# A graph layer with residual and layer norm: 417 edge lists of up to 385 nodes instead of 441 of up to 308

## The reference

```
row, col = src, dst
messages = x[col] @ W.T + b
agg      = segment_sum(messages * agg_weight, row, num_segments=100000)
h        = x + agg
out      = (h - mean(h)) / sqrt(var(h) + 1e-5)      # over the 128 features
```

## Time and profile before

| | |
|---|---|
| median of 3 runs | 845.09 us (844.79 to 850.85) |
| profiled execution | 849.63 us |
| its span | 847.9 us |
| VectorE, TensorE busy | 752.7 us (89%), 721.6 us (85%) |
| ScalarE, GpSimd busy | 635.2 us (75%), 590.1 us (70%) |
| mean granted TensorE clock | 0.965 |

### The profile page before, as it was taken

How to read it: one execution, slowest core, us unless ns; L and a number is a source line. 1 busy time by engine, 2 the same in 40 slices (tenths; PEclk the granted TensorE clock), 3 DMA queues, 4 the chain that set the end, 5 groups by cost and what they waited for, 6 DMA issues and landing times.

```text
span 847.9 us, 22961 instructions
## 1 busy us (share of the span) xinstructions
PE 721.6 (85%) x7822; PEld 540.1 (64%) x7849; DVE 752.7 (89%) x2457; ACT 635.2 (75%) x1592; POOL 590.1 (70%) x601
## 2 busy tenths in 40 slices
PE   4889999999997888888887887888879888888875
PEld 4745555555545667777766766767668677666764
DVE  7989999999966889998988998989899889898985
ACT  2157778777823778887887887888788788878878
POOL 3037777776747777777777777777777777777750
PEclk9999999999998998998999999999999999999998
DMA  2001111111042677777777777777777777777773
GB/s 78 14 27 34 35 39 40 41 39 34 9 150 62 199 240 222 226 232 224 223 228 221 230 238 233 228 222 227 240 229 231 218 232 231 233 224 232 226 223 141
DMA packets 81025, 141.11 MB, mean 166 GB/s; under 512 B 19360, under 2 KB 20396, under 8 KB 80908
## 3 DMA queue, kind: packets, MB, share of 16 engines
q1 hardware_dynamic: 62476, 110.55, 39.1%
q0 software_dynamic: 18432, 29.08, 14.4%
HBM read 87.64 MB, written 51.92 MB: 165 GB/s over the span
## 4 chain that ended last, share of the span: by engine, by line
PE 34%; POOL 21%; DVE 16%; issue 13%; DMA 9%; ACT 7%; POOLq 0%; SPq 0%; ACTq 0%; DVEq 0%
POOL xg L522 20%; PE bank L654 10%; DMA xg<-in_x,table 8%; PE bank L732 7%; ACT y L1100 5%; DVE stats L993 3%; DVE sel L977 2%; DVE rest L975 2%; PE bank L603 2%; PE bank L548 2%; DVE xl L980 2%; PE bank L609 2%; PE bank L702 1%; PE bank L706 1%; PE bank L704 1%
## 5 line engine op out<-in xcount | busy, mean ns | idle before, releaser
L522 POOL DMA_INDIRECT xg<-in_x,table x441 | 445.8, 1011 | 143.5 <-issue 130.1
L1100 ACT ACTIVATE y<-h,shift,rstd 128x128 f32<-128x128 f32 x784 | 321.6, 482 | 78.6 <-DVE shift L1004 78.4
L732 PE MATMUL bank<-wT,aggT 128*128 128x128 f32 x1568 | 237.2, 297 | 0.0
L732 PEld LDWEIGHTS bank<-wT,aggT 128*128 128x128 f32 x1568 | 198.9, 199 | 27.0 <-issue 9.0
L702 PE MATMUL bank<-sel,xg 128*128 128x308 bf16 (+11 forms) x685 | 166.5, 256 | 11.6 <-DVE xl L980 6.3
L477 POOL DMA_INDIRECT place_scratch<-word_col,place_row x135 | 135.7, 1005 | 54.6 <-issue 50.4
L704 PE MATMUL bank<-sel,rest 128*128 128x308 bf16 (+11 forms) x685 | 172.5, 255 | 0.0
L706 PE MATMUL bank<-sel,xl 128*128 128x308 bf16 (+11 forms) x685 | 162.8, 255 | 0.0
L993 DVE BATCH_NORM_STATS2 stats<-h 128x6 f32<-128x256 f32 x392 | 147.6, 418 | 0.2
L986 DVE TENSOR_TENSOR h<-bank,xt 128x512 f32<-128x512 f32 x196 | 133.8, 683 | 13.8 <-PE bank L732 12.9
L975 DVE TENSOR_TENSOR rest<-xg 128x384 f32<-128x384 f32 x196 | 88.9, 454 | 51.8 <-DMA xg<-in_x,table 51.6
(11 more groups left out here) (151 smaller groups left out, 787.8 us busy)
## 6 DMA issues: line engine op xcount, KB each, us to landing
xt<-in_x SPq DMA_DIRECT2D x195, 256.0 KB
out<-y SPq DMA_DIRECT2D x195, 256.0 KB, 2.4
xg<-in_x,table POOLq DMA_INDIRECT x441, 3.5
hi_row<-hi_scratch SPq DMA_DIRECT2D x50, 128.0 KB
place_scratch<-word_col,place_row POOLq DMA_INDIRECT x135
place_scratch<-scattered SPq DMA_DIRECT2D x1, 441.0 KB, 3.4
scattered<-place_scratch SPq DMA_DIRECT2D x1, 441.0 KB, 3.3
src_rows<-in_src SPq DMA_DIRECT2D x1, 192.0 KB
```

The costliest lines, as they stand in the source:

```text
L522: nc.gpsimd.indirect_dma_start(out=xg[:, m, k], out_offset=None, in_=x, in_offset=bass.IndirectOffsetOnAxis(ap=table[:, period * LISTS + k ...
L732: last = nc.tensor.matmul(OUT[u % RO][:, nodes[j]], aggT[:, u % RO, nodes[j]], wT[:], start=False, stop=True, skip_group_check=True)
L1100: nc.scalar.activation(y[:, u, j], h[:, u, j], ACT.Identity, bias=shift[:, u, j:j + 1], scale=rstd[:, u, j:j + 1]).then_inc(s_y, 1)
```

## The change

A period is now 4096 nodes (8 groups) with 17 lists, so a list has 241 nodes of its own instead of 228, and its tail is 144 nodes instead of 80. A selection is 385 columns wide (384 for the seventeenth list) instead of 308 or 307. There are 25 periods; the last has four groups, so only nine of its lists exist, and 417 lists are left. Every loop leaves out lists from number `NB` on. `xg` holds 2 periods and `sel`, `rest` and `xl` one, again 16 and 8 groups, and the waits on `s_sum`, `s_out` and `s_agg` ask for the same groups as before. In the last round GpSimd also fetches the list that ends beyond the last group. The lists that begin in a group are 3, 2, 3, 1 in a period before, and 3, 2, 2, 3, 2, 2, 2, 1 after; those that end in it 2, 2, 2, 3 before, and 2 in seven groups and 3 in the eighth after.

```diff
-    SPAN_G, LISTS = 4, 9
+    SPAN_G, LISTS = 8, 17
     SPAN_N = SPAN_G * GN
-    SPAN_BITS = 11
-    PERIODS = GA // SPAN_G
-    NB = LISTS * PERIODS
-    TAIL = 80
+    SPAN_BITS = 12
+    PERIODS = -(-GA // SPAN_G)
+    TAIL = 144
     FIRST = [-(-SPAN_N * k // LISTS) for k in range(LISTS + 1)]
+    NB = LISTS * (PERIODS - 1) + sum(FIRST[k] < (GA - (PERIODS - 1) * SPAN_G) * GN for k in range(LISTS))
...
-    RX = 4
+    RX = 2
+    XR = 1
...
-        sel = sb("sel", [P, 2, LISTS, SW], bf16)
-        rest = sb("rest", [P, 2, LISTS, D])
-        xl = sb("xl", [P, 2, LISTS, D], bf16)
+        sel = sb("sel", [P, XR, LISTS, SW], bf16)
+        rest = sb("rest", [P, XR, LISTS, D])
+        xl = sb("xl", [P, XR, LISTS, D], bf16)
...
-                    for turn, k in enumerate(LAST_IN[u % SPAN_G]):
+                    mine = LAST_IN[u % SPAN_G]
+                    if g == GA - 1:
+                        mine = [k for k in range(mine[0], LISTS) if period * LISTS + k < NB]
+                    for turn, k in enumerate(mine):
                         if period >= RX:
-                            if turn == 0:
-                                pool.wait_ge(s_sum, g - RX * SPAN_G + 1)
+                            if turn == 0 or k not in LAST_IN[u % SPAN_G]:
+                                pool.wait_ge(s_sum, (period - RX) * SPAN_G + (FIRST[k + 1] - 1) // GN + 1)
                             elif turn == 1:
                                 at_least(pool, s_out, g - RX * SPAN_G - 1)
...
-                    parts = PARTS[g % SPAN_G] if g < GA - 1 else PARTS[g % SPAN_G][:-1]
                     period = g // SPAN_G
-                    return [((period + k // LISTS) % RX, (period + k // LISTS) % 2, k % LISTS, slice(lo, hi), slice(at, at + hi - lo))
-                            for k, lo, hi, at in parts]
+                    return [((period + k // LISTS) % RX, (period + k // LISTS) % XR, k % LISTS, slice(lo, hi), slice(at, at + hi - lo))
+                            for k, lo, hi, at in PARTS[g % SPAN_G] if period * LISTS + k < NB]
...
-                    at_least(dve, s_agg, g - (SPAN_G + 2))
-                    mine = CLASS[u % SPAN_G]
+                    at_least(dve, s_agg, g - (XR * SPAN_G - 2))
+                    mine = [k for k in CLASS[u % SPAN_G] if period * LISTS + k < NB]
```

More of the change, by code:

```diff
@@ L66, in gnn_resnorm_kernel @@
     RO = 4
-    RX = 4
+    RX = 2
+    XR = 1
     EPS = 1e-5
-    assert NS > NB and GA % SPAN_G == 0 and 1 << SPAN_BITS == SPAN_N and 1 << LO_BITS == LO and CA <= KB * P and GN == 512 and NB <= 512 and N <= 1 << 17
+    assert NS > NB and 1 << SPAN_BITS == SPAN_N and 1 << LO_BITS == LO and CA <= KB * P and GN == 512 and NB <= 512 and N <= 1 << 17
     ctx = ExitStack()
@@ L342, in rounds @@
                         stage(g, g % R, g // R, g // SPAN_G, g // SPAN_G % RX, g // SPAN_G // RX)
-        assert SPAN_G == RO and R % SPAN_G == 0
+        assert R % SPAN_G == 0 and max(WIDTH) <= GN
         block = ctx.enter_context(nc.Block())
@@ L693, in aggregate @@
                     if u % SPAN_G < SPAN_G - 1:
-                        pe.wait_ge(s_sel, LISTS * period + sum(len(c) for c in CLASS[:u % SPAN_G + 1]))
+                        pe.wait_ge(s_sel, min(NB, LISTS * period + sum(len(c) for c in CLASS[:u % SPAN_G + 1])))
                     elif last_group:
@@ L973, in select @@
                         dve.wait_ge(s_first[m], 16 * mn + 16)
-                    dve.wait_ge(s_rest[m][u % SPAN_G], (16 * mn + 16) * len([k for k in mine if k]))
-                    V.tensor_tensor(rest[:, m % 2, lists], xg[:, m, lists], top[:, m, lists, :, 1], ALU.subtract).then_inc(s_upper, 1)
+                    dve.wait_ge(s_rest[m][u % SPAN_G], 16 * mn * len([k for k in CLASS[u % SPAN_G] if k]) + 16 * len([k for k in mine if k]))
+                    V.tensor_tensor(rest[:, m % XR, lists], xg[:, m, lists], top[:, m, lists, :, 1], ALU.subtract).then_inc(s_upper, 1)
                     for k in mine:
-                        V.tensor_scalar(sel[:, m % 2, k, 0:WIDTH[k]], iota_win[:, WIN[k]:WIN[k] + WIDTH[k]],
+                        V.tensor_scalar(sel[:, m % XR, k, 0:WIDTH[k]], iota_win[:, WIN[k]:WIN[k] + WIDTH[k]],
                                         table[:, period * LISTS + k, 1:2], None, ALU.is_equal).then_inc(s_sel, 1)
                     dve.wait_ge(s_upper, g + 1)
-                    V.tensor_tensor(xl[:, m % 2, lists], rest[:, m % 2, lists], middle[:, m % 2, lists, :, 1], ALU.subtract).then_inc(s_lower, 1)
+                    V.tensor_tensor(xl[:, m % XR, lists], rest[:, m % XR, lists], middle[:, m % XR, lists, :, 1], ALU.subtract).then_inc(s_lower, 1)
                 def add_x(g, u, n, period, m, mn):
```

2 lines of the change are left out of this document (1 added, 1 removed).

## The result

The changed kernel takes 809.74 us (808.70 to 809.88), the kernel before 845.31 us: ratio 0.956, 95% interval 0.953 to 0.959. It is faster, by 35.6 us. The forecast of 815.7 us had the sign and the pacing engine right, but its range, 811 to 824 us, does not reach down to the measured time. Two extra figures are needed to read the traces: the profiled execution after took 808.70 us (span 807.0), 1 us under its median, and that of before 849.63, 4.3 us over its median. So the two traces differ by 40.9 us, the medians by 35.6.

A forecast was written before the change was run, and what follows sets the result against it. GpSimd, issuing gathers without a stop, was taken to bound the main stage. Gathers -30.1, sorting stage -0.5 and drain +1.2 us sum to -29.4, taking the median from 845.09 to 815.7 us; range 811 to 824.

The forecast's parts named there:

- 24 gathers: GpSimd, main stage: 441 gathers become 417, saving 30.1 us (bounds 29 to 31.6).
- The width is hidden: VectorE, main stage: with wider selections it needs 2.68 us a group, covered by GpSimd's 2.79.
- Rings and waits: Main stage: rings hold as many groups and waits ask for the same groups as before, so cost nothing.
- (1): Rival, main stage: VectorE or TensorE takes over the pace; median 818 to 828 us; chance 0.13.
- (2): Rival: the VectorE, ScalarE and TensorE loop already needs the present pace; gain under 8 us, 838 to 845; chance 0.06.
- (3): Rival: 385-wide selections leave the fast form on VectorE, 0.24 us more each; +45 us, about 890; chance 0.04.
- (4): Rival: lists overflow and the serial branch runs, taking over 3500 us; chance 0.01.
- Several signs: Things to check in the profile after: gather period, last gather's start, waits of VectorE and TensorE, selection times, merge start.
- this excess ... stays: GpSimd's gathers: the 26 us beyond 0.952 us each stays, so each removed gather saves only 1.25 us.
- the drain: After the last gather: TensorE sets the pace for some six groups, 0.2 us more each, +1.2 us.
- the stage before: Sorting stage ahead of the gathers: narrower matmuls and one-hot tiles, scatters unchanged; -0.5 us (0 to 1.4 gain).

The follow-up runs named there:

- before_more: Kernel before plus one more gather per group into an unread spare tile, 637 gathers in all: 1090.4 us, ratio 1.290 to the kernel before.
- after_more: Changed kernel plus one more gather per group into an unread spare tile, 613 gathers in all: 1053.4 us, ratio 1.246 to the kernel before.
- narrow_17: Changed kernel with the tail of 80 instead of 144 (417 lists, 321-column selections); two runs, ratios 0.957 and 0.959 to the kernel before.
- form_only: Changed kernel with 18 lists and tail 80: the same 441 lists as the kernel before, in periods of 8 groups; ratios 0.996, 0.997, 0.996 to it.
- before_24_less: Kernel before with 24 of its 441 gathers left out, all else kept; three runs, ratios 0.973, 0.974 and 0.978 to the kernel before.
- wide_only: Changed kernel with 18 lists instead of 17 and its tail of 144 (441 lists): 1101.3 us, ratio 1.000 to the kernel before.
- after_again: Changed kernel run again without an edit: 1076.3 us, ratio 0.956 to the kernel before on the same chip.
- before_again: Kernel before run again without an edit: 1102.1 us, ratio 1.002.
- before_cut: Kernel before with both splits made list by list, 441 short ones each instead of 196: ratio 1.003.
- before_joined: Kernel before with the split xl moved ahead of the selections, right behind the split rest: ratio 1.002.

## Why the prediction was right in kind and too small

**Right.** GpSimd sets the pace, and 24 gathers are most of the gain: shown by before_more against after_more, by narrow_17 against form_only for the lists as a whole, and by before_24_less in part. The width is hidden on VectorE's own path: it needs 2.66 us a group (forecast 2.68), a selection 336 ns (331); the waits left are 21.1 us ("some 20"). Rings and waits changed nothing that GpSimd waits for. Rivals (1), (2) and (3) did not happen, and (4) neither: 417 gathers, no serial branch. Several signs missed their numbers: the period was 1.299 us, not 1.31 to 1.32; the last gather came 40.1 us earlier, not 30; TensorE's waits for ScalarE fell by 44 us, not 30; the merge started at 236.8 us, not 237 to 238.

**Wrong: the term "this excess ... stays".** I took 24 x 1.25 and held the 26 us that gathers take beyond 0.952 constant. It fell. Between the two traces it went from 441 x 0.059 = 26.0 us to 417 x 0.042 = 17.5, 8.5 us. On the medians less of that is left: 35.6 less 30.1 (the 24 gathers at 1.25), 1.4 and 0.8 leaves 3.3 us. The other 5.2 us are about what the two profiled executions stood off their medians (4.3 above and 1.0 below); that it was the gathers' excess that differed there is inferred, since the other executions have no trace. What lengthens a gather can be seen in the trace of before. GpSimd, then VectorE:

```profile
564.58 1.34 POOL L522 DMA_INDIRECT xg<-in_x,table  x1 [0.30 <-issue]
566.23 0.95 POOL L522 DMA_INDIRECT xg<-in_x,table  x1 [0.30 <-issue]
...
568.74 1.19 POOL L522 DMA_INDIRECT xg<-in_x,table  x1 [0.30 <-issue]
```

```profile
564.55 0.55 DVE L980 TENSOR_TENSOR xl<-rest 128x384 bf16<-128x384 f32 x1
...
566.02 0.69 DVE L986 TENSOR_TENSOR h<-bank,xt 128x512 f32<-128x512 f32 x1
...
568.55 0.55 DVE L975 TENSOR_TENSOR rest<-xg 128x384 f32<-128x384 f32 x1
```

The gather at 564.58 starts when a split has 0.52 us to go and is 0.39 too long; the one at 568.74 has 0.36 to go, 0.24 too long; the one at 566.23 starts during `add_x` and has its 0.95. A gather that starts in a split is longer by what is left of it, less 0.12 us: to within 0.03 us this fits 90 of the 94 gathers in the trace of before that start with more than 0.16 us of a split to go, and 56 of 58 after. Selections, which are shorter, hold a gather too, as the trace of after shows (GpSimd, then VectorE):

```profile
777.87 1.05 POOL L526 DMA_INDIRECT xg<-in_x,table  x1 [0.30 <-issue]
```

```profile
777.13 0.97 DVE L980 TENSOR_SCALAR sel<-iota_win,table 128x385 bf16<-128x385 f16 x3
778.01 0.54 DVE L983 TENSOR_TENSOR xl<-rest 128x384 bf16<-128x384 f32 x1
```

This gather starts with 0.23 us of the last selection to go and is 0.10 too long. By the start times in the whole traces, the excess goes with these starts:

| gathers that start | before | after |
|---|---|---|
| in a split | 122, 19.6 us | 124, 11.2 us |
| at most 0.16 us ahead of a split that then holds them | 12, 6.0 us | 5, 2.2 us |
| in a selection, 0.06 us or more too long | 1, 0.1 us | 38, 3.7 us |
| in a selection, less than that | 23, 0.3 us | 33, 0.5 us |
| all others | 283, 0.0 us | 217, -0.1 us |
| all | 441, 26.0 us | 417, 17.5 us |

132 gathers that start in `add_x` in the trace of before have 0.9 us in all (six stand in both counts). So "it stays" failed as the difference of two changes: the splits' part fell by 12.2 us, the selections' part rose by 3.8, where the prediction had at most 1. The rise goes with the width: the group of 0.06 us and more has 0.1 us in form_only and 0.4 in narrow_17, but 2.9 in wide_only and 2.6 in after_again.

Why the splits held less is argued, not shown. Splits of three lists (0.48 us from start to start) fell from 98 of each kind to 49, those of two (0.34) rose from 49 to 123, those of one fell from 49 to 24. If both the chance that a gather hits a split and its loss grow with the length, then with (length - 0.12) squared as weight eight groups have 4 x 0.130 + 2 x 0.048 + 2 x 0.006 = 0.63 before and 2 x 0.130 + 5 x 0.048 + 0.006 = 0.51 after, a fifth less, 5 us of 26. From before_more to after_more the splits' part did fall by a sixth (19.2 to 15.9 us), but narrow_17, grouped like the changed kernel, has 24.2 us of it, and the same weights give form_only 6% less, 1.5 us, where its excess is 5.0 us below that of before_again. before_cut and before_joined, made to move the excess, did not move it as expected. With the same lengths the splits' part is 13.4 us in one trace and 24.2 in another, on another chip, so it must also matter how the rhythms of the two engines meet; what sets that stays open.

The Trainium skill ("SBUF — State Buffer", section "SBUF: two separate sides") has the rule that I missed in its full form: beside fast modes, a VectorE operation with two SBUF inputs excludes a GpSimd operation that reads SBUF. The trace agrees for the splits (two SBUF inputs, up to 0.56 us) and for `add_x` (one input from PSUM, none). That the start of an indirect DMA is such a reading operation is inferred here from the overlaps. Of `tensor_tensor` the Trainium skill infers the opposite (same page, section "Who interferes with whom"), that it leaves the making of a DMA's descriptors alone; the 90 of 94 gathers decide against that. The rule's other half, which I had weighed for the selections, fits as well, with 3.8 us where I had at most 1; whether these selections run in such a mode no trace shows.

**Wrong: the drain, forecast +1.2 us.** It was -0.8. TensorE's rounds did get longer (`h` at 789.03, 791.59 and 794.16 us, 2.56 a round, forecast 2.55), but only three rounds waited for it, not six (four in the trace of before):

```profile
789.03 0.69 DVE L989 TENSOR_TENSOR h<-bank,xt 128x512 f32<-128x512 f32 x1 [0.20 <-ACT y L1103]
...
791.59 0.69 DVE L989 TENSOR_TENSOR h<-bank,xt 128x512 f32<-128x512 f32 x1 [1.08 <-PE bank L735]
...
794.16 0.69 DVE L989 TENSOR_TENSOR h<-bank,xt 128x512 f32<-128x512 f32 x1 [0.78 <-PE bank L735]
...
796.30 0.69 DVE L989 TENSOR_TENSOR h<-bank,xt 128x512 f32<-128x512 f32 x1 [0.66 <-PE bank L735]
```

and VectorE was less far behind at the last gather: its last selections start 5.1 us after it (785.58 - 780.48), in the trace of before 6.2 (826.80 - 820.59).

**Wrong: the stage before, forecast -0.5 us.** It was -1.4, the whole of what the read-back allowed. With two ends known to 1.4 us I had taken the lower third for no reason in the rows. TensorE and VectorE, not the scatters, ended last in both.

Together: 3.3 + 2.0 + 0.9 = 6.2 us, the distance from -29.4 to -35.6 (the 3.3 is what remains when the others are taken off, so the sum closes by construction). The range failed because its lower end let each gather that goes take its share of the excess with it and nothing beyond that, with no gain in the drain.

## What to carry to other kernels

An engine with little busy time can set the pace: look at the period from start to start, and whether its pauses are "issue". The number of its instructions is then the price. Wider work on another engine is free on that engine as long as it still waits for the slow one, but it can hold up the slow engine's instructions, here by some 4 us. If instructions come in two lengths, find what the long ones meet before holding their excess constant.

## What the runs showed of the hardware

An indirect DMA that starts while VectorE runs a tensor_tensor on two SBUF operands waits for its end (0.39 us longer with 0.52 us to go; 90 of 94 such starts fit). One that starts during a 385-wide 16-bit selection does so too (0.10 us longer with 0.23 to go). Three short tensor_tensor operations without a gap sometimes held it as one, sometimes not. The same kernel took 845 us on some chips and 1101 to 1127 us on four others, where TensorE paused, at a granted clock of 0.85 to 0.90 for the kernel before; the cause is open. The ratio of the two kernels was 0.956 in both conditions, though different engines waited.
